# Head softmax: GpSimd's order of issue, weighing and quarter sums, and ScalarE's copy of eight heads behind the unit's own second exponential

## The chip, the cores and the metric

One core of a Trainium2 chip runs the whole program. The metric is the device time in microseconds of one execution; runs of this kernel are compared by their medians. Below, TensorE (PE) multiplies, VectorE (DVE) and ScalarE (ACT) work elementwise and reduce, GpSimd (POOL) does elementwise work and issues some DMAs, SyncE (SP) issues the other DMAs.

## What is computed

One transformer-like block on x of 4 x 1024 tokens by 128 features: banded attention, a mixture-of-experts feed-forward, then the attention of this case, and the feed-forward again. The attention of this case takes its softmax over the heads (axis 1), not over the keys:

```python
def _L0_attn_b_ref(x, Wq, bq, Wk, bk, Wv, bv, Wo, bo):
    B, S, E = x.shape
    H = N_HEADS          # 16
    D = E // H           # 8
    q = (x @ Wq.T + bq).reshape(B, S, H, D)
    k = (x @ Wk.T + bk).reshape(B, S, H, D)
    v = (x @ Wv.T + bv).reshape(B, S, H, D)
    scores = jnp.einsum('bqnd,bknd->bnqk', q, k) / jnp.sqrt(jnp.float32(D))
    attn = jax.nn.softmax(scores, axis=1)
    out = jnp.einsum('bnqk,bknd->bnqd', attn, v)
    out = out.transpose(0, 2, 1, 3).reshape(B, S, E)
    return out @ Wo.T + bo
...
x = x + _L0_attn_b_ref(_layernorm(x, axis=-1), ...)
```

So for each pair of query and key the sixteen scores are exponentiated and divided by their sum, and nothing is summed over keys but the weighted values.

## The kernel before

The stage is one function, `head_softmax_attention`. It has 4 batches of 8 query tiles (128 queries), and 8 key tiles for each query tile. One query tile against one key tile is a **unit**: 256 of them, in order. Each engine has its own program for the whole stage, a plain loop over the units written out by hand, and runs its instructions strictly in that order; semaphores alone tie the engines together. A unit's scores are [128 keys, 16 heads x 128 queries], held in PSUM in two halves of 64 queries (h = 0 and 1), two banks each. A half's banks are used again by the next unit's same half.

What one unit does, with the lines of the kernel before:

- TensorE makes the scores of a half (L890) and VectorE takes their maximum over the heads, negated (L1115, `head_shift`). TensorE adds it to the scores in place (L912, semaphore `shifted`), and ScalarE takes the exponential of the half into `ex` (L1069), a ring of 6 units.
- The sum over the 16 heads goes by halving. ScalarE copies heads 0 to 7 of the unit's `ex` into `half` (L1032, `copy_heads`). GpSimd issues a DMA that adds heads 8 to 15 onto them in place (L847, `add_halves`, 512 KB counted read and written). GpSimd adds heads 4 to 7 onto 0 to 3 (L853, `add_quarters`). TensorE sums the last four by four matmuls with the identity (L922, `denominator_of`) into the bank `den`; the profile shows them as eight.
- ScalarE turns the denominator into its reciprocal by a logarithm (L1038) and two exponentials: `recp` in PSUM for VectorE (L1041) and `recip` in SBUF for GpSimd (L1043). VectorE weighs the first ten heads (L1122), GpSimd the other six (L859, `weigh_rest`).
- TensorE multiplies the weighed exponentials with the values, 16 matmuls by head, 32 in the profile (L905, `attend`).

The denominator of unit u - 4 is made while unit u's scores are, and unit u - 5 is attended to in the same turn. TensorE's order in a turn is: maximum matmul of (u, 0), scores of (u, 1), denominator of u - 4, scores of (u + 1, 0), maximum matmul of (u, 1), attend to u - 5, and then extra work by key tile (`ahead`): with key tile 0 the next query tile's projection, with 2 the keys and with 4 the values of the next batch, with 6 the output product of the query tile before (L928, L929). The scores of a half wait for the exponential that last read its banks. VectorE's order: reduction of (u, 1), of (u + 1, 0), weighing of u - 4, and extra work: with key tile 1 the low part of the queries (L1102), with 3 that of the keys (L1102), with 5 the values, with 7 the residual sum, with 0 and 2 statistics. ScalarE's order in a turn is: first exponential, copy of unit u - 1, with key tile 5 the copy of the attention's result (L1048), the three instructions of the reciprocal of u - 4, second exponential, and with key tile 1 and 3 the high part of queries and keys (L1027), for which L1102 waits. The keys, and values, of a next batch are made in the first three batches alone.

GpSimd's loop has one step a turn, with s its number: weigh unit s - 4, issue the DMA of unit s - 1, add the quarters of unit s - 2. The DMA waits for the copy, the quarters for the DMA's landing, the weighing for `recip`.

`exps` and `copies` give the value that the semaphore `ex_ready` has when an exponential or a copy is done; all three kinds of ScalarE's instructions raise it in their order.

Of the kernel before, what the change touches and what calls it, by code (L numbers as in the profile page):

```python
# [715 lines left out]
def head_softmax_attention(nc, c, x, mv, ht, q_dram, k_dram, k_first, zero_f16, zero_f32):  # L716
# [8 lines left out]
    LAG, RING, SUMS = 4, 6, 4  # L725
    ON_DVE = 10
    BY_DMA = 0
    ALL = B * NQ * BT
# [4 lines left out]
    with Mem(nc, "head") as m:  # L733
# [34 lines left out]

        def exps(unit, h):

            return 3 * unit + 2 if h == 1 else max(3 * unit, 1)

        def copies(unit):

            return 3 * unit + (4 if unit < ALL - 1 else 3)

        def turned(k):

            return (den, recp, outp)[k % 3]

        def chunks(eng, chunk_of):

            for b in range(B):
                chunk_of(b, 0, 0)
                for pair in range(0, (NQ - 2) // 2):
                    chunk_of(b, pair * 2 + 1, 1)
                    chunk_of(b, pair * 2 + 2, 0)
                chunk_of(b, NQ - 1, 1)

        def is_chunk(b, q, n):  # L790

            return isinstance(q, int) and b * NQ + q == n
# [47 lines left out]
        @block.gpsimd  # L840
        def _(pool):
            m.start(pool, "pool")

            def add_halves(unit):

                pool.wait_ge(ex_ready, ONE + copies(unit))
                pool.dma_start(half[:, unit % SUMS, :, :], ex[:, unit % RING, 8:16, :], accum_op=ALU.add).then_inc(summed[unit % 2], 16)  # L847

            def add_quarters(unit):

                pool.wait_ge(summed[unit % 2], (unit // 2 + 1) * 16)
                hf = half[:, unit % SUMS, :, :]
                pool.tensor_tensor(hf[:, 0:4, :], hf[:, 0:4, :], hf[:, 4:8, :], ALU.add).then_inc(quarter_ready, 1)  # L853

            def weigh_rest(unit):

                pool.wait_ge(copy_ready, ONE + unit + 1)
                e = ex[:, unit % RING, ON_DVE:NH, :]
                pool.tensor_tensor(e, e, recip[:, unit % 2, :][:, None, :].broadcast_to([P, NH - ON_DVE, P]),  # L859
                                   ALU.mult).then_inc(rest_ready, 1)  # L860

            for step in range(ALL + LAG):
                if step >= LAG:
                    weigh_rest(step - LAG)
                if 0 < step <= ALL:
                    add_halves(step - 1)
                if 1 < step <= ALL + 1:
                    add_quarters(step - 2)

        @block.tensor  # L870
        def _(pe):
# [141 lines left out]
        @block.scalar  # L1013
        def _(act):
            m.start(act, "act")
            act.wait_ge(rstd_chain, ONE + 1)
            act.activation(std[:, :], std[:, :], ACT.Sqrt).then_inc(std_ready, 1)
            act.preload_act_table_set("natural_log_exp_and_others")

            def high_turned(k):  # L1020

                act.wait_ge(turned_ready, ONE + k + 1)
                act.activation(xnT[:, 0, k * BLK:(k + 1) * BLK], turned(k)[:, :], ACT.Copy).then_inc(xhigh_ready, 1)

            def high_part(parts, bank, cols, u):

                return act.activation(parts, bank[:, None, :].broadcast_to([P, 2, cols]), ACT.Identity, bias=c["b_bias"][:, u:u + 1])  # L1027

            def copy_heads(unit):

                act.wait_ge(ex_ready, ONE + exps(unit, 1))
                act.activation(half[:, unit % SUMS, BY_DMA:8, :], ex[:, unit % RING, BY_DMA:8, :], ACT.Copy).then_inc(ex_ready, 1)  # L1032

            def reciprocal_of(unit):

                act.wait_ge(copy_ready, ONE + unit)
                act.wait_ge(den_ready, ONE + unit + 2)
                act.activation(lnd[:, :], den[:, 0:P], ACT.Ln).then_inc(ln_done, 1)  # L1038
                act.wait_ge(ln_done, ONE + unit + 1)
                act.wait_ge(prob_ready, ONE + unit + 1)  # L1040
                act.activation(recp[:, 0:P], lnd[:, :], ACT.Exp, scale=-1.0).then_inc(recip_ready, 1)  # L1041
                act.wait_ge(rest_ready, ONE + unit)
                act.activation(recip[:, unit % 2, :], lnd[:, :], ACT.Exp, scale=-1.0).then_inc(copy_ready, 1)  # L1043

            def copy_out(n):
                act.wait_ge(av_done, ONE + n * BT + BT + RING - 1)
                act.wait_ge(out_ready, ONE + n)
                act.activation(outT[:, :], outp[:, 0:P], ACT.Copy).then_inc(outT_ready, 1)  # L1048

            def ahead(b, q, kt):  # L1050
                n = b * NQ + q
                if kt == 1 and not is_chunk(b, q, LAST):
                    act.wait_ge(q_ready, ONE + n + 2)
                    act.wait_ge(q_written, ONE + (n + 1) * 16)
                    high_part(parts_q[:, 0:3:2, :], proj[:, at_q], P, 0).then_inc(q_high, 1)
                if kt == 3 and b < B - 1:
                    act.wait_ge(k_ready, ONE + n + HALVES + 1)
                    act.wait_ge(k_written, ONE + (n + HALVES) * 16)
                    high_part(parts_k[:, 0:2, :], proj[:, at_k], P, 1).then_inc(k_high, 1)

            def chunk_of(b, q, par):
                n, first = b * NQ + q, is_chunk(b, q, 0)
                for kt in range(BT):
                    unit = n * BT + kt
                    for h in range(2):
                        act.wait_ge(shifted, ONE + 2 * unit + h + 1)
                        if h == 0:
                            act.wait_ge(av_done, ONE + unit)
                        act.activation(ex[:, unit % RING, :, h * QS:(h + 1) * QS].rearrange("p (a g) w -> p g a w", g=NG),  # L1069
                                       score[:, h, :, :].rearrange("p k (g a w) -> p (k g) a w", a=GH, w=QS),  # L1070
                                       ACT.Exp, scale=SCALE / ASCALE ** 2).then_inc(ex_ready, 1)
                        if h == 0 and unit > 0:
                            copy_heads(unit - 1)
                        if h == 0 and kt == LAG + 1 and not first:
                            copy_out(n - 1)
                        if h == 0 and not (first and kt < LAG):
                            reciprocal_of(unit - LAG)
                    ahead(b, q, kt)

            high_turned(0)  # L1080
            high_turned(1)
            for i in range(HALVES):
                act.wait_ge(k_ready, ONE + i + 1)
                high_part(parts_first[:, i, 0:2, :], score[:, 0, i, :], BLK, 1).then_inc(k_high, 1)
                if i == 0:
                    act.wait_ge(q_ready, ONE + 1)
                    high_part(parts_q[:, 0:3:2, :], score[:, 1, 0, 0:P], P, 0).then_inc(q_high, 1)
            for k in range(2, NBLK):
                high_turned(k)
            chunks(act, chunk_of)  # L1090
            copy_heads(ALL - 1)
            for kt in range(BT - LAG, BT):
                reciprocal_of(LAST * BT + kt)
            copy_out(LAST)
# [690 lines left out]
```

## Time and profile before

| | us |
|---|---|
| three runs | 1952.0, 1943.28, 1948.12 |
| their median | 1948.12 |
| the profiled execution's own time | 1951.87 |
| its span, first to last instruction | 1950.1 |
| busy in it: TensorE matmuls | 1835.9 (94%) |
| VectorE | 1653.7 (85%) |
| ScalarE | 1434.7 (74%) |
| GpSimd | 1443.5 (74%) |
| first and last exponential of the stage start at | 547.8, 1619.0 |
| granted clock of TensorE, 548 to 580 | 0.74 of full |
| the same, 900 to 934, 1200 to 1234 and 1500 to 1534 | 1.00 |

The shares are means over four stages with different limits, and the head softmax stage is a little over half of the span. Busy shares don't say what it waits for, since four engines are above 85% in it. The timeline does: it gives the start of each instruction, and two starts on one engine or on two are a link whose length can be read. A bracket at a row's end says how long the engine was idle before it and what released it. Instructions of one engine often overlap a little (the end of one lies behind the start of the next), so links are best measured from start to start. PE is the matmul itself, PEld the loading of its weights.

### The profile page before, as it was taken

Reading aid. Unit: us, or ns where it says so; the run is one execution under the profiler, and the core shown is the slowest. Engines: PE = TensorE matmul, PEld = TensorE weight load, DVE = VectorE, ACT = ScalarE, POOL = GpSimd, SP = SyncE. Lnnn points to the kernel's source line nnn. Section 1 sums busy time; section 2 is a strip of 40 time slices with the busy share of each in tenths; the row PEclk is TensorE's granted clock in tenths of the full one; section 3 lists DMA queues with packets and bytes.
Section 4 is the critical chain, followed back from the end, with each engine's and each line's share of the span. In section 5 each row is a group of like instructions: output and inputs, shape, how many; then the busy total and the mean of one; then the engine's idle time right before and its main releaser. Section 6 shows DMA issues by size and latency. Waiting matters only on the chain. (4 is left out here: it accounts for less than half of the span.)

```text
span 1950.1 us, 52397 instructions
## 1 busy us (share of the span) xinstructions
PE 1835.9 (94%) x20664; PEld 1154.3 (59%) x20664; DVE 1653.7 (85%) x2601; ACT 1434.7 (74%) x2473; POOL 1443.5 (74%) x1180
## 2 busy tenths in 40 slices
PE   5999799999789999999999999999999997999998
PEld 3666644444346666666666666666666665544443
DVE  6777688887679999999999999999999995788776
ACT  4566456666568888888888888888888884566665
POOL 6245256565349999999999989989999997456565
PEclk8999699999879999999999999999999997899999
DMA  6644176765267777777777667777767772677673
GB/s 162 195 110 105 27 150 140 135 141 113 81 140 141 143 136 140 136 139 139 139 136 142 133 134 144 139 136 139 137 125 138 135 134 56 130 151 154 124 133 56
DMA packets 156741, 253.07 MB, mean 130 GB/s; under 512 B 54736, under 2 KB 86368, under 8 KB 155760
## 3 DMA queue, kind: packets, MB, share of 16 engines
q0 software_dynamic: 36864, 134.23, 36.7%
q1 hardware_dynamic: 114112, 112.89, 26.7%
q8 instruction: 164, 2.69, 0.6%
q10 hardware_dynamic: 5520, 2.60, 0.5%
q14 instruction: 81, 0.66, 0.1%
HBM read 96.95 MB, written 18.55 MB: 59 GB/s over the span
## 5 line engine op out<-in xcount | busy, mean ns | idle before, releaser
L1115 DVE TENSOR_REDUCE head_shift<-head_score 128x64 bf16<-128x1024 f32 x512 | 625.8, 1222 | 74.4 <-PE head_score L890 48.2
L1069 ACT ACTIVATE head_ex<-head_score 128x1024 f32<-128x1024 f32 x512 | 521.1, 1018 | 121.5 <-PE head_score L912 120.9
L859 POOL TENSOR_TENSOR head_ex<-head_ex,head_recip 128x768 f32<-128x768 f32 x256 | 491.0, 1918 | 7.3 <-ACT head_recip L1043 6.6
L1371 POOL TENSOR_TENSOR ffn_sw<-ffn_sg,ffn_wide 128x512 f32<-128x512 f32 x256 | 324.9, 1269 | 218.4 <-ACT ffn_sg L1482 203.7
L853 POOL TENSOR_TENSOR head_half<-head_half 128x512 f32<-128x512 f32 x256 | 359.4, 1404 | 70.1 <-DMA head_half<-head_ex 67.8
L1122 DVE TENSOR_TENSOR head_ex<-head_ex,head_recp 128x1280 f32<-128x1280 f32 x256 | 378.2, 1477 | 10.0 <-ACT head_recp L1041 10.0
L912 PE MATMUL head_score<-head_shift,c_identb 128*128 128x512 bf16 x1024 | 311.7, 386 | 17.0 <-DVE head_shift L1115 11.7
L890 PE MATMUL head_score<-att_b_HB,att_b_GR 96*128 96x256 f16 x2048 | 312.4, 275 | 1.4 <-ACT head_ex L1069 1.4
L922 PE MATMUL head_den<-head_half,c_ident 128*128 128x128 f32 x2048 | 281.6, 281 | 20.2 <-POOL head_half L853 19.3
L847 POOL DMA_DIRECT2D head_half<-head_ex x256 | 251.2, 981 | 47.3 <-ACT head_half L1032 47.3
L905 PE MATMUL head_outp<-head_ex,att_b_vs 128*32 128x128 f32 x8192 | 277.4, 277 | 0.0
L922 PEld LDWEIGHTS head_den<-head_half,c_ident 128*128 128x128 f32 x2048 | 251.6, 193 | 39.4 <-POOL head_half L853 36.1
L905 PEld LDWEIGHTS head_outp<-head_ex,att_b_vs 128*32 128x32 f32 x8192 | 210.2, 110 | 107.0 <-issue 106.7
L1032 ACT ACTIVATE head_half<-head_ex 128x1024 f32<-128x1024 f32 x256 | 268.6, 1049 | 0.0
L1616 DVE TENSOR_TENSOR ffn_hidden<-ffn_sw,ffn_up 128x512 f32<-128x512 f32 x256 | 178.2, 696 | 93.1 <-POOL ffn_sw L1371 86.6
L1482 ACT ACTIVATE ffn_sg<-ffn_gate 128x512 f32<-128x512 f32 x272 | 162.4, 597 | 115.8 <-PE ffn_gate L116 114.7
L890 PEld LDWEIGHTS head_score<-att_b_HB,att_b_GR 96*128 96x128 f16 x2048 | 189.0, 98 | 88.2 <-ACT head_ex L1069 40.1
L1487 ACT ACTIVATE ffn_h_parts<-ffn_hidden 128x512 f16<-128x512 f32 x272 | 162.5, 597 | 97.4 <-DVE ffn_hidden L1616 90.6
L1624 DVE TENSOR_TENSOR ffn_h_parts<-ffn_hidden,ffn_h_parts 128x512 f16<-128x512 f32 x272 | 186.0, 684 | 0.1
L912 PEld LDWEIGHTS head_score<-head_shift,c_identb 128*128 128x128 bf16 x1024 | 66.9, 98 | 107.7 <-DVE head_shift L1115 83.9
L114 PE MATMUL ffn_down<-ffn_h_parts,c_down_parts 128*128 128x512 f16 x272 | 103.2, 379 | 3.3 <-DVE ffn_h_parts L1624 3.3
L114 PE MATMUL ffn_up<-ffn_xnT,c_up_parts 128*128 128x512 f16 x272 | 104.0, 382 | 0.6 <-DVE ffn_hidden L1616 0.3
(265 smaller groups left out, 2538.7 us busy)
## 6 DMA issues: line engine op xcount, KB each, us to landing
head_half<-head_ex POOLq DMA_DIRECT2D x256, 512.0 KB, 5.0
ffn_wide<-pair_weights SPq DMA_DIRECT2D x256, 256.0 KB, 9.7
band_v_windows<-a_values SPq DMA_DIRECT2D x24, 192.0 KB, 4.8
att_b_vs<-in_zero_f SPq DMA_DIRECT2D x2, 2176.0 KB, 10.0
a_keys<-band_parts_k SPq DMA_DIRECT2D x12, 295.5 KB, 2.5
att_a_HB<-a_keys SPq DMA_DIRECT2D x48, 73.9 KB
a_queries<-band_parts_q SPq DMA_DIRECT2D x12, 271.5 KB, 2.9
att_a_GR<-a_queries SPq DMA_DIRECT2D x12, 271.5 KB
```

The costliest lines, as they stand in the source:

```text
L847: pool.dma_start(half[:, unit % SUMS, :, :], ex[:, unit % RING, 8:16, :], accum_op=ALU.add).then_inc(summed[unit % 2], 16)
L853: pool.tensor_tensor(hf[:, 0:4, :], hf[:, 0:4, :], hf[:, 4:8, :], ALU.add).then_inc(quarter_ready, 1)
L859: pool.tensor_tensor(e, e, recip[:, unit % 2, :][:, None, :].broadcast_to([P, NH - ON_DVE, P]), ALU.mult).then_inc(rest_ready, 1)
L890: last = pe.matmul(score[:, h, g // 2, (g % 2) * GH * QS:(g % 2 + 1) * GH * QS].rearrange("p (a w) -> p a w", a=GH), GR[:, buf, g, kt * P: ...
L905: last = pe.matmul(outp[g * 32:(g + 1) * 32, 0:P], vs[:, buf * BT + kt, at:at + 32], ex[:, unit % RING, i, :], start=(kt == 0 and n4 == 0) ...
L912: last = pe.matmul(score[:, h, k, :].rearrange("p (a w) -> p a w", a=NH // 2), c["identb"][:, :], shift[:, h, :][:, None, :].broadcast_to( ...
L922: last = pe.matmul(den[:, 0:P], c["ident"][:, :], half[:, unit % SUMS, k, :], start=(i == 0), stop=(i == len(SLABS) - 1))
L1032: act.activation(half[:, unit % SUMS, BY_DMA:8, :], ex[:, unit % RING, BY_DMA:8, :], ACT.Copy).then_inc(ex_ready, 1)
L1069: act.activation(ex[:, unit % RING, :, h * QS:(h + 1) * QS].rearrange("p (a g) w -> p g a w", g=NG), score[:, h, :, :].rearrange("p k (g a ...
L1115: dve.tensor_reduce(shift[:, h, :], score[:, h, :, :].rearrange("p k (a w) -> p w k a", a=NH // 2), AX.XY, ALU.max, negate=True).then_inc( ...
L1122: dve.tensor_tensor(e, e, recp[:, 0:P][:, None, :].broadcast_to([P, ON_DVE, P]), ALU.mult).then_inc(prob_ready, 1)
L1371: pool.tensor_tensor(sw[:, unit % 2, :], sg[:, unit % 2, :], wide[:, k % 2, i, :], ALU.mult).then_inc(sw_ready, 1)
```

## The change

ScalarE's copy of a unit's heads 0 to 7 moves: from behind the first exponential of the next unit to behind the second exponential of its own unit, ahead of the `ahead` work and of the next unit's first exponential. The counts in `exps` and `copies` follow that order, and the last unit's separate copy goes. GpSimd's step is now: issue the DMA of unit s - 1, weigh unit s - 4, add the quarters of unit s - 2. At its end the last unit's quarters come ahead of the last three weighings. Nothing else is changed; no instruction is added or taken away.

```diff
         def exps(unit, h):
 
-            return 3 * unit + 2 if h == 1 else max(3 * unit, 1)
+            return 3 * unit + h + 1
 
         def copies(unit):
 
-            return 3 * unit + (4 if unit < ALL - 1 else 3)
+            return 3 * unit + 3
...
-            for step in range(ALL + LAG):
+            for step in range(ALL + 1):
+                if step > 0:
+                    add_halves(step - 1)
                 if step >= LAG:
                     weigh_rest(step - LAG)
-                if 0 < step <= ALL:
-                    add_halves(step - 1)
-                if 1 < step <= ALL + 1:
+                if step > 1:
                     add_quarters(step - 2)
+            add_quarters(ALL - 1)
+            for unit in range(ALL + 1 - LAG, ALL):
+                weigh_rest(unit)
...
-                        if h == 0 and unit > 0:
-                            copy_heads(unit - 1)
+                        if h == 1:
+                            copy_heads(unit)
                         if h == 0 and kt == LAG + 1 and not first:
                             copy_out(n - 1)
                         if h == 0 and not (first and kt < LAG):
...
             chunks(act, chunk_of)
-            copy_heads(ALL - 1)
             for kt in range(BT - LAG, BT):
```

ScalarE, around the units with key tile 0 to 2 of a query tile, before. `head_ex` is written by the exponentials (L1069), `head_half` by the copy (L1032), `head_parts_q` is the high part of the queries; x2 stands for a second exponential and the next unit's first:

```order
L1069 ACTIVATE head_ex<-head_score 128x4x4x64 x2
L1032 ACTIVATE head_half<-head_ex 128x1024
L1038 ACTIVATE head_lnd<-head_den 128x128
L1041 ACTIVATE head_recp<-head_lnd 128x128
L1043 ACTIVATE head_recip<-head_lnd 128x128
L1069 ACTIVATE head_ex<-head_score 128x4x4x64
L1027 ACTIVATE head_parts_q<-head_proj,c_b_bias 128x2x128
L1069 ACTIVATE head_ex<-head_score 128x4x4x64
L1032 ACTIVATE head_half<-head_ex 128x1024
L1038 ACTIVATE head_lnd<-head_den 128x128
L1041 ACTIVATE head_recp<-head_lnd 128x128
```

And with the change (there the lines are L1072 for the exponentials, L1035 for the copy, L1041, L1044 and L1046 for the reciprocal, L1030 for the parts):

```order
L1035 ACTIVATE head_half<-head_ex 128x1024
L1072 ACTIVATE head_ex<-head_score 128x4x4x64
L1041 ACTIVATE head_lnd<-head_den 128x128
L1044 ACTIVATE head_recp<-head_lnd 128x128
L1046 ACTIVATE head_recip<-head_lnd 128x128
L1072 ACTIVATE head_ex<-head_score 128x4x4x64
L1035 ACTIVATE head_half<-head_ex 128x1024
L1030 ACTIVATE head_parts_q<-head_proj,c_b_bias 128x2x128
L1072 ACTIVATE head_ex<-head_score 128x4x4x64
L1041 ACTIVATE head_lnd<-head_den 128x128
L1044 ACTIVATE head_recp<-head_lnd 128x128
L1046 ACTIVATE head_recip<-head_lnd 128x128
```

The copy has gone from behind the first of two adjacent exponentials to between them, and the parts of the queries stand behind it.

GpSimd, the end of its loop, before (L847 is the DMA, L859 the weighing, L853 the quarters, here and with the change; a step began with L859):

```order
L859 TENSOR_TENSOR head_ex<-head_ex,head_recip 128x768
L847 DMA head_half<-head_ex 128x1024
L853 TENSOR_TENSOR head_half<-head_half 128x512
L859 TENSOR_TENSOR head_ex<-head_ex,head_recip 128x768
L853 TENSOR_TENSOR head_half<-head_half 128x512
L859 TENSOR_TENSOR head_ex<-head_ex,head_recip 128x768 x2
```

And with the change:

```order
L853 TENSOR_TENSOR head_half<-head_half 128x512
L847 DMA head_half<-head_ex 128x1024
L859 TENSOR_TENSOR head_ex<-head_ex,head_recip 128x768
L853 TENSOR_TENSOR head_half<-head_half 128x512 x2
L859 TENSOR_TENSOR head_ex<-head_ex,head_recip 128x768 x3
```

The DMA stands ahead of the weighing instead of behind it; at the end two quarter sums are adjacent and three weighings follow them, where before the last quarter sum had a weighing ahead of it and two behind.

## Rows read from the trace of the kernel before

**Rows 1.** The line of the exponentials: durations in ns, first and last start.

```profile
L1069 ACT ACTIVATE head_ex<-head_score x512: 1002/1025/1028, 547.8 to 1619.0; 128x1024 f32<-128x1024 f32 x171
```
**Rows 2.** Timeline, 920 to 926.5, a unit with key tile 1; start, duration, engine.

```profile
920.20 0.59 PE L912 MATMUL head_score<-head_shift,c_identb 128*128 128x512 bf16 x2
...
920.83 1.02 ACT L1069 ACTIVATE head_ex<-head_score 128x1024 f32<-128x1024 f32 x1 [0.69 <-PE head_score L912]
...
921.05 0.29 DVE L1132 BATCH_NORM_STATS2 head_stats<-x_tokens 128x6 f32<-128x128 f32 x1
...
921.27 2.56 DVE L1115 TENSOR_REDUCE head_shift<-head_score 128x64 bf16<-128x1024 f32 x2
...
921.75 1.05 ACT L1032 ACTIVATE head_half<-head_ex 128x1024 f32<-128x1024 f32 x1
...
921.96 0.60 PE L890 MATMUL head_score<-att_b_HB,att_b_GR 96*128 96x256 f16 x4
...
922.55 0.60 PE L912 MATMUL head_score<-head_shift,c_identb 128*128 128x512 bf16 x2
...
922.70 0.27 ACT L1038 ACTIVATE head_lnd<-head_den 128x128 f32<-128x128 f32 x1
...
923.42 1.00 ACT L1069 ACTIVATE head_ex<-head_score 128x1024 f32<-128x1024 f32 x1
...
923.74 1.48 DVE L1122 TENSOR_TENSOR head_ex<-head_ex,head_recp 128x1280 f32<-128x1280 f32 x1
...
924.10 0.60 PE L912 MATMUL head_score<-head_shift,c_identb 128*128 128x512 bf16 x2
...
924.32 0.46 ACT L1027 ACTIVATE head_parts_q<-head_proj,c_b_bias 128x256 f16<-128x256 f32 x1
...
924.47 0.39 PEld L890 LDWEIGHTS head_score<-att_b_HB,att_b_GR 96*128 96x128 f16 x4 [0.26 <-ACT head_ex L1069]
...
925.13 0.34 DVE L1102 SCALAR_TENSOR_TENSOR head_parts_q<-head_proj,c_b_bias,head_parts_q 128x128 f16<-128x128 f32 x1
```
**Rows 3.** Timeline, 910.5 to 916: the output product, and scores that came late.

```profile
910.98 0.49 PE L928 MATMUL head_proj<-c_b_bo,c_ident 128*128 128x128 f32 x2
...
911.53 0.59 PE L912 MATMUL head_score<-head_shift,c_identb 128*128 128x512 bf16 x2
...
913.82 0.60 PE L890 MATMUL head_score<-att_b_HB,att_b_GR 96*128 96x256 f16 x4
...
914.26 0.60 PE L912 MATMUL head_score<-head_shift,c_identb 128*128 128x512 bf16 x2
...
914.46 1.23 DVE L1115 TENSOR_REDUCE head_shift<-head_score 128x64 bf16<-128x1024 f32 x1 [0.64 <-PE head_score L890]
...
915.60 1.48 DVE L1122 TENSOR_TENSOR head_ex<-head_ex,head_recp 128x1280 f32<-128x1280 f32 x1
```
**Rows 4.** Waits, 580 to 1616: engine, line, releaser; total, times, longest.

```profile
POOL head_half L853 <- DMA head_half<-head_ex: 67.2, 87, 2.0
...
PEld head_den L922 <- POOL head_half L853: 28.8, 62, 1.6
...
PE head_den L922 <- POOL head_half L853: 13.1, 26, 1.3
```
**Rows 5.** GpSimd's quarters (durations in ns, min/median/max) and the landing of L847's DMA.

```profile
L853 POOL TENSOR_TENSOR head_half<-head_half x256: 1257/1377/1592, 559.8 to 1630.0; 128x512 f32<-128x512 f32 x128
...
DMA to landing us min/median/max: 4.5/5.0/6.9
```
**Rows 6.** Timeline, 1618.5 to 1641: the end of the stage.

```profile
1618.97 1.00 ACT L1069 ACTIVATE head_ex<-head_score 128x1024 f32<-128x1024 f32 x1
...
1620.01 1.06 ACT L1032 ACTIVATE head_half<-head_ex 128x1024 f32<-128x1024 f32 x1
...
1631.37 2.07 PE L922 MATMUL head_den<-head_half,c_ident 128*128 128x128 f32 x8 [1.62 <-POOL head_half L853]
...
1633.37 6.08 PE L905 MATMUL head_outp<-head_ex,att_b_vs 128*32 128x128 f32 x160
```
## The prediction

> **Words.** A unit is one key tile against one query tile; there are 256, eight to a query tile, and I number the eight 0 to 7. "First" and "second" mean the two halves of a unit (h = 0, 1). "Maximum matmul" is L912 (it adds the negated maximum to the scores), "scores" L890, "reduction" L1115, "copy" L1032, "quarters" L853, "parts" L1027 with VectorE's L1102. Every link below is a start-to-start time in us.
>
> **What bounds the kernel now.** The change touches only the head softmax stage, so I read first how long that takes: its 512 exponentials run from 547.8 to 1619.0 [rows 1], and with 2.6 between a unit's two exponentials (923.42 - 920.83) [rows 2] the 255 steps take 1068.6, 4.19 a unit, 33.52 for eight. Then the timeline of a unit in which nothing waited for GpSimd [rows 2]: from first maximum matmul to the next unit's, 920.20 to 924.10, is 3.90. This is a loop of TensorE and VectorE: second scores, the reduction at 921.27, the second maximum matmul 1.28 after it at 922.55, the weighted sum, and round. ScalarE is not in it: its first exponential starts 0.63 behind the matmul that releases it, then copy, logarithm, two reciprocals, second exponential. Units 0, 2, 4 and 6 have extra TensorE work (0.55 for the output product, 911.53 - 910.98) [rows 3]; units 0, 1, 3, 5 and 7 have extra VectorE work (0.22: 921.27 - 921.05) [rows 2]. What is left of the 4.19 is read from the waits: the denominator's matmul waited 13.1 for GpSimd's quarters and its weight load 28.8 [rows 4], partly the same waits, and GpSimd itself 67.2 in 87 waits for the DMA that adds the upper heads. So the loop bounds, GpSimd's lateness adds to it, and ScalarE has room, but only where its work stands now.
>
> **What the change removes.** The copy of a unit ends behind the same unit's second exponential, and GpSimd issues its DMA before it weighs. A unit's DMA then goes out nearly a unit earlier, and the quarters have one weighing more to wait behind. The landing takes 4.5 to 6.9, 5.0 in the middle [rows 5], and now has over a step of GpSimd for it. I take all waits of rows 4 for gone: worth 13.1 at the least (the matmul's own) and 28.8 at the most. The Trainium skill ("DMA: Bandwidth & Descriptors", section "Anatomy of one DMA — SWDGE (gpsimd) path") gives 2.0 us and 436 KB per us, which for these 512 KB would be an estimate of 3.2; were that so, the 87 waits would not be there and this term would be nought. The trace has 5.0, so the term stays.
>
> The tail gains too. The last copy starts at 1620.01 and takes 1.06 [rows 6], 5.0 for the DMA [rows 5] and 1.38 for the quarters [rows 5] bring the last denominator to 1627.45 instead of 1631.37: 3.9 less, since 160 matmuls wait behind it (1633.37). GpSimd's three last weighings now stand behind these quarters, but TensorE reaches their units one after another in 6.08, so I cost them at nothing; were that cover gone, about a weighing each would come back.
>
> **What the change adds: a new loop.** The copy now stands between a unit's second exponential and the next unit's first. The first question is room: the two maximum matmuls that release these exponentials are 1.55 apart (924.10 - 922.55) [rows 2]. The copy needs its own exponential finished: behind the last one it started 1.04 later (1620.01 - 1618.97) [rows 6], where an instruction that needs nothing of its predecessor starts 0.92 later (921.75 - 920.83) [rows 2]. And 0.95 after the copy the next can start (922.70 - 921.75). That is 1.99 where there is 1.55: the next first exponential is 0.44 late, and only 0.08 of that is free, since the scores that wait for it start at 921.96 and it can be read 1.05 after its start (924.47 - 923.42), at 921.88. The second exponential, freed of the copy ahead of it, does start earlier, but only until its own matmul's 0.63.
>
> So a loop through ScalarE closes, from second maximum matmul to second maximum matmul: 0.63 to the exponential, 1.04 to the copy, 0.95 to the next first exponential, 1.05 to the scores that overwrite its bank, 0.44 to the maximum matmul behind them (914.26 - 913.82) [rows 3]. Sum **4.11**, against 3.90.
>
> The Trainium skill ("Perfetto Trace Analysis", section "Per-engine timelines") says that an instruction on ScalarE may begin when the one ahead has finished executing, while its semaphore moves only after memory has acknowledged the bytes. The trace agrees, 0.92 against 1.04. Had the copy started after 0.92, the loop would be 3.99 and the final sum about 8 less.
>
> Where the parts are made (unit 1 for queries; unit 3 for keys, in the first three of four batches: 32 - 1 and 24 times, 55 in all), they stand behind the copy on ScalarE, and VectorE's L1102 waits for them. Now VectorE takes it right behind its weighing (925.13, 1.39 after 923.74) [rows 2]. Then: 0.63 + 1.04 + 0.95, 0.46 for the parts, 0.05 to hand over (924.47 is 0.05 behind the end of the exponential, 923.42 + 1.00), 0.22 on VectorE, 1.28 to the maximum matmul: **4.63**. The next reductions are queued behind that waiting instruction, and TensorE waits for them.
>
> Where VectorE has extra work (units 5, 7, 0) the late scores meet it: 0.64 from scores to second reduction (914.46 - 913.82), 1.14 to the weighing (915.60), 1.39, 0.22, 1.28, less the 0.44 from scores to maximum: **4.23**. Unit 6, with the output: 3.90 + 0.55 = **4.45**, above the ScalarE loop. Units 2 and 4: 4.11.
>
> **The sum.** Eight units: 2 x 4.63 + 3 x 4.23 + 4.45 + 2 x 4.11 = 34.62. In the last batch, without keys and values, units 3 and 5 fall to 4.11: 33.98. Before: 33.52. So 24 query tiles lose 1.10 and 8 lose 0.46: 30.1. The waits on the quarters are inside the 33.52 and are not in the new sum, so their gain is already counted. Less 3.9 at the end: +26.2. The profiled execution took 1951.87, which makes 1978.1; against the median of the runs, 1948.12, it makes **1974**. Other stages don't change.
>
> **Rivals.**
> A, faster: the lateness of the first exponential is swallowed, the waits on the quarters go. For it: TensorE has the denominator's matmuls to do before those scores. Against it: 0.08 of cover where 0.44 is needed [rows 2]. It decides once the copy needs under 1.63 in all. It gives 13.1 + 3.9 = 17 to 28.8 + 3.9 = 33 less: 1931 to 1915; I take 1925. The Trainium skill's 3.2 for the DMA (same page and section, an estimate) would leave it the tail alone.
> B, nothing: ordinary units swallow it, in part because quarters no longer push TensorE, and only the 55 units with parts pay 4.63 - 4.11 = 0.52, 28.6 in all. With the gains of A this is +12 to -4, in the middle 1952.
> C, slower still: the chain lengthens and something keeps the denominator late as well, so that the 13.1 isn't won: 1987 (with the 28.8, 2003). Against it: quarters would be done almost a unit before they are needed.
> That the change doesn't do what it says (a DMA no earlier, because GpSimd now waits for the copy) is part of C; the copy ends 1.0 into the next unit, while GpSimd comes to it later.
>
> **Chances.** Forecast 0.58; A 0.18; B 0.14; C 0.10. The runs can tell about 0.5%, 10 us, from no change. Forecast and C are slower by more; of B 0.11 lie within and 0.03 above; of A 0.17 are faster and 0.01 within. Faster 0.17, same 0.12, slower 0.71. The range runs from 1950, the middle of B, to 1995, between the two prices of C: 0.58 + about half of B + most of C, the forecast's own errors included (its links are read to 0.01 to 0.05, and 0.05 in a link that every unit has is 13 us).
>
> **What would show it.** Right: 4.3 a unit between first exponentials; the copy about 1.04 behind the second exponential, the first exponential with no idle time ahead of it, mostly 0.95 behind the copy; GpSimd's 67.2 for the DMA and TensorE's waits for quarters near nought; in their place TensorE waiting for the exponential, VectorE waiting for scores (more than before), and L1102 waiting for ScalarE some 0.5 in units 1 and 3; the last denominator 6.4 behind the end of the last copy. Wrong: first exponentials that still follow their matmul by 0.63 with scores on time (A); L1102 alone late (B); waits on quarters still there (C).

## The result, and the profile after

The changed kernel takes 1984.65 us (median of 4 runs, 1983.31 to 1985.94) against 1949.37 for the kernel before in the same comparison: a ratio of 1.0191, 95% interval 1.0165 to 1.0218. It is slower by 35 us. The two profiled spans are 1950.1 and 1982.5, 32.4 apart. The forecast was 1974, in a range of 1950 to 1995.

The waits of the kernel after, from 580 to 1650 (engine, line, what it waited for; us in total, times, longest). In its numbering the exponentials are L1072, the copy L1035, the maximum matmul L915, the scores L893, the denominator L925, the reduction L1117, VectorE's low part L1104, GpSimd's weighing L859:

```profile
POOL head_ex L859 <- ACT head_recip L1046: 104.2, 186, 1.0
PEld head_score L893 <- ACT head_ex L1072: 98.7, 217, 0.8
...
DVE head_shift L1117 <- PE head_score L893: 64.8, 194, 0.5
...
PE head_score L893 <- ACT head_ex L1072: 52.7, 141, 0.6
ACT head_lnd L1041 <- PE head_den L925: 11.4, 31, 0.4
DVE head_parts_q L1104 <- ACT head_parts_q L1030: 11.3, 30, 0.5
...
DVE head_parts_k L1104 <- ACT head_parts_k L1030: 7.4, 23, 0.3
```

Nothing in it waits for GpSimd's quarters or for its DMA any more, where [rows 4] had 67.2, 28.8 and 13.1. In their place TensorE's scores wait for the exponential that reads their banks, 52.7 by the matmul itself. Before, the same view (580 to 1616) had no such wait of the matmul, and for its weight load

```profile
PEld head_score L890 <- ACT head_ex L1069: 34.6, 118, 0.4
```

GpSimd now waits for ScalarE instead of the DMA: it has become early.

The line of the exponentials, which answers to [rows 1] (durations in ns, first and last start):

```profile
L1072 ACT ACTIVATE head_ex<-head_score x512: 1002/1023/1028, 548.1 to 1656.9; 128x1024 f32<-128x1024 f32 x171
```

It spans 1108.8 where it spanned 1071.2: the stage's loop alone is 37.6 longer. What stands behind the last exponential got shorter, so the loss is all in the loop.

Two turns of the loop after, in order of time (start, duration, engine). The first is a unit with key tile 1, as in [rows 2]:

```profile
974.75 0.60 PE L915 MATMUL head_score<-head_shift,c_identb 128*128 128x512 bf16 x2
...
975.39 1.03 ACT L1072 ACTIVATE head_ex<-head_score 128x1024 f32<-128x1024 f32 x1 [0.28 <-PE head_score L915]
...
976.45 1.06 ACT L1035 ACTIVATE head_half<-head_ex 128x1024 f32<-128x1024 f32 x1
...
977.41 0.46 ACT L1030 ACTIVATE head_parts_q<-head_proj,c_b_bias 128x256 f16<-128x256 f32 x1
977.76 1.01 ACT L1072 ACTIVATE head_ex<-head_score 128x1024 f32<-128x1024 f32 x1
977.90 0.35 DVE L1104 SCALAR_TENSOR_TENSOR head_parts_q<-head_proj,c_b_bias,head_parts_q 128x128 f16<-128x128 f32 x1 [0.38 <-ACT head_parts_q L1030]
978.17 2.54 DVE L1117 TENSOR_REDUCE head_shift<-head_score 128x64 bf16<-128x1024 f32 x2
...
978.83 0.61 PE L893 MATMUL head_score<-att_b_HB,att_b_GR 96*128 96x256 f16 x4 [0.60 <-ACT head_ex L1072]
...
979.44 0.61 PE L915 MATMUL head_score<-head_shift,c_identb 128*128 128x512 bf16 x2
```

From second maximum matmul (974.75) to the next (979.44) are 4.69: 0.64, 1.06, 0.96 on ScalarE, 0.49 to L1104, 0.27, 1.27. VectorE stood idle 0.38 for the parts, TensorE 0.60 for the exponential. The second turn is one with key tile 5, without parts:

```profile
992.46 0.60 PE L915 MATMUL head_score<-head_shift,c_identb 128*128 128x512 bf16 x2
...
993.09 1.03 ACT L1072 ACTIVATE head_ex<-head_score 128x1024 f32<-128x1024 f32 x1 [0.24 <-PE head_score L915]
...
994.15 1.06 ACT L1035 ACTIVATE head_half<-head_ex 128x1024 f32<-128x1024 f32 x1
...
995.12 1.00 ACT L1072 ACTIVATE head_ex<-head_score 128x1024 f32<-128x1024 f32 x1
...
996.18 0.61 PE L893 MATMUL head_score<-att_b_HB,att_b_GR 96*128 96x256 f16 x4 [0.24 <-ACT head_ex L1072]
...
996.67 0.61 PE L915 MATMUL head_score<-head_shift,c_identb 128*128 128x512 bf16 x2
```

Here the loop closes through ScalarE: 0.63 to the exponential, 1.06 to the copy, 0.97 to the next first exponential, 1.06 to the scores that wait for it, 0.49 to the maximum matmul, 4.21. ScalarE's first exponential has no idle time ahead of it; before, it had 0.69.

The loop has also become quite regular. The parts of the queries come once in eight units; on ScalarE they start at 907.91, 942.66 and 977.41, which is 34.75 and 34.75 apart. Before, eight units took 33.5 in the mean and anything between 32.8 and 34.7.

The end of the stage, to be held against [rows 6]:

```profile
1657.99 1.06 ACT L1035 ACTIVATE head_half<-head_ex 128x1024 f32<-128x1024 f32 x1
...
1664.46 1.26 POOL L853 TENSOR_TENSOR head_half<-head_half 128x512 f32<-128x512 f32 x1 [0.67 <-DMA head_half<-head_ex]
...
1666.07 1.91 PE L925 MATMUL head_den<-head_half,c_ident 128*128 128x128 f32 x8 [0.52 <-ACT head_lnd L1041]
...
1667.91 4.57 PE L908 MATMUL head_outp<-head_ex,att_b_vs 128*32 128x128 f32 x160
...
1672.55 0.28 ACT L1051 ACTIVATE head_outT<-head_outp 128x128 f32<-128x128 f32 x1 [3.65 <-PE head_outp L908]
```

From the last exponential (1656.93) to the copy of the result (1672.55) are 15.62; before they were 20.56 (1618.97 to 1639.53). That is 4.9 gained.

### The profile page after: what moved, and what is told of

Its sections match the earlier page's. It is cut to its first block and busy times, and to the rows that moved or that the text cites. A ratio compares the mean times of both kernels' runs of the same rounds, so it can differ in the third digit from the quotient of the medians.

```text
span 1982.5 us, 52397 instructions
## 1 busy us (share of the span) xinstructions
PE 1838.1 (93%) x20664; PEld 1163.1 (59%) x20664; DVE 1656.9 (84%) x2601; ACT 1471.1 (74%) x2473; POOL 1435.8 (72%) x1180
## 5 line engine op out<-in xcount | busy, mean ns | idle before, releaser
L1117 DVE TENSOR_REDUCE head_shift<-head_score 128x64 bf16<-128x1024 f32 x512 | 625.2, 1221 | 88.1 <-PE head_score L893 75.0
L1072 ACT ACTIVATE head_ex<-head_score 128x1024 f32<-128x1024 f32 x512 | 520.7, 1017 | 104.2 <-PE head_score L915 104.0
L859 POOL TENSOR_TENSOR head_ex<-head_ex,head_recip 128x768 f32<-128x768 f32 x256 | 467.7, 1827 | 111.9 <-ACT head_recip L1046 107.5
L893 PE MATMUL head_score<-att_b_HB,att_b_GR 96*128 96x256 f16 x2048 | 315.2, 277 | 62.0 <-ACT head_ex L1072 56.7
L853 POOL TENSOR_TENSOR head_half<-head_half 128x512 f32<-128x512 f32 x256 | 326.0, 1274 | 0.7 <-DMA head_half<-head_ex 0.7
L915 PE MATMUL head_score<-head_shift,c_identb 128*128 128x512 bf16 x1024 | 312.3, 387 | 3.9 <-DVE head_shift L1117 3.7
L893 PEld LDWEIGHTS head_score<-att_b_HB,att_b_GR 96*128 96x128 f16 x2048 | 181.6, 98 | 182.0 <-ACT head_ex L1072 107.9
L925 PE MATMUL head_den<-head_half,c_ident 128*128 128x128 f32 x2048 | 273.1, 277 | 4.2 <-POOL head_half L853 3.7
L1035 ACT ACTIVATE head_half<-head_ex 128x1024 f32<-128x1024 f32 x256 | 270.8, 1058 | 8.1
L908 PE MATMUL head_outp<-head_ex,att_b_vs 128*32 128x128 f32 x8192 | 275.9, 276 | 0.0
L908 PEld LDWEIGHTS head_outp<-head_ex,att_b_vs 128*32 128x32 f32 x8192 | 208.3, 110 | 106.6 <-issue 106.5
L847 POOL DMA_DIRECT2D head_half<-head_ex x256 | 221.8, 866 | 53.6 <-ACT head_half L1035 50.3
L925 PEld LDWEIGHTS head_den<-head_half,c_ident 128*128 128x128 f32 x2048 | 250.8, 193 | 8.2 <-POOL head_half L853 4.9
L915 PEld LDWEIGHTS head_score<-head_shift,c_identb 128*128 128x128 bf16 x1024 | 74.0, 98 | 70.5 <-DVE head_shift L1117 59.1
```

The lines of the kernel that those rows point to most:

```text
L893: last = pe.matmul(score[:, h, g // 2, (g % 2) * GH * QS:(g % 2 + 1) * GH * QS].rearrange("p (a w) -> p a w", a=GH), GR[:, buf, g, kt * P: ...
L908: last = pe.matmul(outp[g * 32:(g + 1) * 32, 0:P], vs[:, buf * BT + kt, at:at + 32], ex[:, unit % RING, i, :], start=(kt == 0 and n4 == 0) ...
L915: last = pe.matmul(score[:, h, k, :].rearrange("p (a w) -> p a w", a=NH // 2), c["identb"][:, :], shift[:, h, :][:, None, :].broadcast_to( ...
L925: last = pe.matmul(den[:, 0:P], c["ident"][:, :], half[:, unit % SUMS, k, :], start=(i == 0), stop=(i == len(SLABS) - 1))
L1117: dve.tensor_reduce(shift[:, h, :], score[:, h, :, :].rearrange("p k (a w) -> p w k a", a=NH // 2), AX.XY, ALU.max, negate=True).then_inc( ...
```

## The experiments

The theory (S) is the forecast's: the copy's new place closes a loop through ScalarE that every unit pays, and more where parts stand behind the copy; GpSimd's new order only takes waits away. Rival G: GpSimd's order is what costs. Rival P: only the 55 units with parts cost, the others swallow the copy. All ratios are against the kernel before, run beside each on the same chip (median 1949.47 us beside the first four runs below, 1950.04 beside the last two).

**One part each.** The first kernel is the one before with GpSimd's new loop alone:

```diff
-            for step in range(ALL + LAG):
+            for step in range(ALL + 1):
+                if step > 0:
+                    add_halves(step - 1)
                 if step >= LAG:
                     weigh_rest(step - LAG)
...
+            add_quarters(ALL - 1)
+            for unit in range(ALL + 1 - LAG, ALL):
+                weigh_rest(unit)
```

The second is the one before with the new place of the copy alone, with the counts in `exps` and `copies` that go with it and without the last unit's separate copy (not shown):

```diff
-                        if h == 0 and unit > 0:
-                            copy_heads(unit - 1)
+                        if h == 1:
+                            copy_heads(unit)
```

> GpSimd's new order (issue, weigh, quarters last) with ScalarE's copy where it was before. Theory S (the copy's place closes a loop through ScalarE; GpSimd's order only takes waits away): the waits for quarters vanish, 4.12 us a unit instead of 4.19, the tail 4 to 5 us shorter, together 1926 us. Rival G (GpSimd's order is what costs: its weighing now stands behind a DMA that waits for the copy, so six heads are weighed late): about as slow as the change, 1985. Rival P (only the 55 units with parts behind the copy cost) expects the same as S here.

Measured: 1930.31 us, ratio 0.9914 (0.9891 to 0.9937). Its line of the exponentials, and GpSimd's quarters with what they waited for and who waited for them:

```profile
L1072 ACT ACTIVATE head_ex<-head_score x512: 1002/1023/1026, 546.8 to 1600.0; 128x1024 f32<-128x1024 f32 x171
```

```profile
L853 POOL TENSOR_TENSOR head_half<-head_half x256: 1263/1561/2507, 558.7 to 1608.2; 128x512 f32<-128x512 f32 x128
its engine sat idle before it (us, times) until:
  DMA head_half<-head_ex: 0.7, 1
who waited for it (us, times):
  PEld head_den L925: 5.6, 3
```

The loop is 1053.2 long instead of 1071.2, 18 less, which is 4.12 a unit as expected. The DMA wait, 67.2 before from 580 to 1616, is 0.7 in the whole stage, and TensorE waits for quarters only at the very end. The tail is 18.04 (1599.99 to 1618.03) instead of 20.56: 2.5, not 4 to 5, of the gain. GpSimd's order gains; G is out for this half.

> ScalarE's copy behind the unit's own second exponential, GpSimd in its order of before. S: the loop as slow as with the whole change, 34.75 us for eight units, since the quarters have time enough in the longer turn; the tail as before, so 1985 + 5 = 1990 us. G: no slower than before, 1949 or less. P: 1990 as well.

Measured: 1989.2 us, ratio 1.0216 (1.019 to 1.0242). Its exponentials and its wait for the DMA:

```profile
L1069 ACT ACTIVATE head_ex<-head_score x512: 1002/1024/1027, 548.9 to 1657.5; 128x1024 f32<-128x1024 f32 x171
```

```profile
  DMA head_half<-head_ex: 31.7, 56
```

The loop is 1108.6 long; the whole change has 1108.8. So with the copy in its new place GpSimd's order no longer moves the loop, though GpSimd still waits 31.7 for DMAs in the old order: the longer turn covers it. What the order does then is to shorten the tail from 20.05 to 15.62. Alone each half is -19 and +40; together they are +35 and not +21, because the 18 that GpSimd's order is worth in the loop can't be had behind a slower loop.

**The length of the copy.** The forecast says that copy and hand-over need 1.99 of ScalarE where 1.63 would be swallowed. Taking the copy to half its heads should bring it under that:

```diff
...
+            pool.memset(half[:, :, 4:8, :], 0.0).then_inc(half_clear, 1)
+            pool.wait_ge(half_clear, ONE + 1)
             for step in range(ALL + 1):
...
-                act.activation(half[:, unit % SUMS, BY_DMA:8, :], ex[:, unit % RING, BY_DMA:8, :], ACT.Copy).then_inc(ex_ready, 1)
+                act.activation(half[:, unit % SUMS, 0:4, :], ex[:, unit % RING, 0:4, :], ACT.Copy).then_inc(ex_ready, 1)
```

> The change, but ScalarE copies 4 heads instead of 8 (GpSimd clears the other four once at the start of the stage, so the denominator leaves out work and is not the reference's). The copy should take about 0.6 instead of 1.06 us, so that copy and hand-over need some 1.55 us against the 1.63 that are free. S: the loop through ScalarE falls to about 3.7 and no longer bounds; TensorE and VectorE bound at 4.12, 1928 us. P: units with parts still pay, 0.52 x 55 less 0.43 x 55, about 1935. G: no effect, 1985.

> Control for the run before it: the kernel before with the same four-head copy (and the same part of the denominator left out). S: the copy is not on the path there, so at most a few us: 1944 to 1950 us. If it gains as much as the four-head copy does in the change, the copy's length was binding in both and its place is not the cause.

Measured: 1937.15 us in the change, ratio 0.9948 (0.9927 to 0.9969), and 1949.16 in the kernel before, ratio 1.0004 (0.9987 to 1.0021). A turn without parts of the first of the two (L1075 is the exponential, L1038 the copy, L918 the maximum matmul):

```profile
905.58 1.03 ACT L1075 ACTIVATE head_ex<-head_score 128x1024 f32<-128x1024 f32 x1 [0.15 <-PE head_score L918]
...
906.48 0.60 PE L918 MATMUL head_score<-head_shift,c_identb 128*128 128x512 bf16 x2
906.63 0.63 ACT L1038 ACTIVATE head_half<-head_ex 128x512 f32<-128x512 f32 x1
...
907.17 1.00 ACT L1075 ACTIVATE head_ex<-head_score 128x1024 f32<-128x1024 f32 x1
```

From second to first exponential are 1.59 (1.05 and 0.54), against 2.03 in the turn at 993.09 of the change. That is under the 1.63, and the exponential comes 0.69 behind its matmul instead of the usual 0.63. 47 us of the change's time are gone; the same shortening in the kernel before is worth nothing. So it is the copy in that place, not the copy's length as such. The run stays 7 us above the kernel with GpSimd's order alone, which S had at nothing, so that P's 1935 lies nearer to it than S's 1928. What is left is in the units with parts, where 0.36 stands between copy and exponential. The scores still waited 9.3 us for the exponential, in 53 waits: 30 behind the parts of the queries and 23 behind those of the keys, and none elsewhere.

```profile
PE head_score L896 <- ACT head_ex L1075: 9.3, 53, 0.2
```

**The parts.** The change with `copy_heads(unit)` moved from ahead of `ahead(b, q, kt)` to behind it:

```diff
-                        if h == 1:
-                            copy_heads(unit)
                         if h == 0 and kt == LAG + 1 and not first:
                             copy_out(n - 1)
                         if h == 0 and not (first and kt < LAG):
                             reciprocal_of(unit - LAG)
                     ahead(b, q, kt)
+                    copy_heads(unit)
```

> The change, with the parts of queries and keys ahead of the copy on ScalarE instead of behind it, in 55 units. S (the copy's place costs in every unit, and more where parts stand behind it): these units fall from 4.63 to 0.63 + 0.92 + 0.42 + 0.95 + 1.05 + 0.44 = 4.41 us, 12 less in all, 1973 us, and L1102 no longer waits for ScalarE. Rival P (the whole loss was in these 55 units, the others swallow the copy): about 1949. If nothing changes, the links of units 1 and 3 were put together wrongly.

Measured: 1968.94 us, ratio 1.0094 (1.0059 to 1.013); 15.7 less than the change, 12 expected. ScalarE in a unit with key tile 1:

```profile
968.38 1.02 ACT L1072 ACTIVATE head_ex<-head_score 128x1024 f32<-128x1024 f32 x1 [0.29 <-PE head_score L915]
969.30 0.47 ACT L1030 ACTIVATE head_parts_q<-head_proj,c_b_bias 128x256 f16<-128x256 f32 x1
969.65 1.06 ACT L1035 ACTIVATE head_half<-head_ex 128x1024 f32<-128x1024 f32 x1
970.60 1.02 ACT L1072 ACTIVATE head_ex<-head_score 128x1024 f32<-128x1024 f32 x1
```

2.22 between the exponentials instead of 2.37 (975.39 to 977.76): the parts start 0.92 behind the exponential because they need nothing of it, and the copy then has its input ready. P is out: 19 of the 35 us stay when the parts no longer wait. These units now turn in 4.38, 4.41 expected, and nothing waits for the parts any more. S holds in both its terms.

**A version that beats both.** GpSimd's order alone is faster than both kernels. I took the loop of TensorE and VectorE for what bounds it, with VectorE a little late from its extra work in units 0, 2 and 4. So I gave GpSimd one more head to weigh:

```diff
-    ON_DVE = 10
+    ON_DVE = 9
```

> GpSimd's new order alone, and VectorE weighs 9 heads, GpSimd 7 (10 and 6 before). With the quarters on time the loop of TensorE and VectorE is what is left, 3.91 a unit, and VectorE's lateness by its extra work in units 0, 2, 4 (0.15, 0.22, 0.16 us). The weighing of 9 heads should take 0.13 less, so up to 0.4 us of 33.05 for eight units, 32 times: 13 us less than that kernel's 1930, 1917. GpSimd gets 0.3 us more a unit and has about 0.4 free; if it has less than that, its quarters or its weighing come late and the time is 1930 or more.

Measured: 1952.25 us, ratio 1.001 (0.9993 to 1.0026), 22 slower than the kernel it was made from. GpSimd's weighing (durations in ns, min/median/max), what waited for it between 600 and 1560, and one unit's values matmuls (L908):

```profile
L859 POOL TENSOR_TENSOR head_ex<-head_ex,head_recip x256: 2081/4066/4277, 567.9 to 1633.2; 128x896 f32<-128x896 f32 x128
```

```profile
PEld head_outp L908 <- POOL head_ex L859: 5.2, 33, 0.2
```

```profile
905.69 4.01 POOL L859 TENSOR_TENSOR head_ex<-head_ex,head_recip 128x896 f32<-128x896 f32 x1
...
909.03 1.36 PE L908 MATMUL head_outp<-head_ex,att_b_vs 128*32 128x128 f32 x32
```

VectorE's weighing did shrink as expected (1.34 instead of 1.48 in its rows), but GpSimd's median record went from 2.13 to 4.07 for one head more. Records on GpSimd overlap in this kernel, so their sum is not its busy time: from start to start, weighing to quarters, it is 2.06 in the median and 2.11 in the mean (2.05 to 3.25) with seven heads, 1.79 with six, and the elements alone would make 2.09. But the end of the record counts for TensorE: the weighing above ends at 909.70, and only then does TensorE load the heads that GpSimd weighed (its first weights at 909.75). The 32 matmuls take 1.2 to 1.4 in 170 of the 229 units that can be told apart in that window, where they take 1.1 in every unit of the kernel with ten heads, in which nothing waits for the weighing. Eight units take 33.5 instead of 33.05. So the seventh head costs because its weighing is done too late for TensorE. The room I saw, 0.4 a unit, was an estimate of GpSimd's free time and said nothing of when TensorE needs its result. Why a weighing is done 4.0 after its start, when the next instruction starts after 2.05, stays open.

## Why the prediction was right

**The direction and the mechanism.** The step on which all rests, that copy and hand-over need 1.99 between two exponentials whose matmuls are 1.55 apart with 0.08 to spare, held. The loop after goes round by the links that were named, and the run with a shorter copy undoes the loss while the control has none to undo. The forecast had 26 us, and the medians are 35 apart, so the loss is larger than was said.

**The links.** Predicted and measured for the turn through ScalarE: 0.63 and 0.63, 1.04 and 1.06, 0.95 and 0.97, 1.05 and 1.06, 0.44 and 0.49; 4.11 and 4.21 in the turn shown, where VectorE's extra work is a part of the last link (the forecast had 4.23 for that unit). With parts 4.63 and 4.69. The sum for eight units was 34.62 and is 34.75. Unit by unit, from second exponential to second exponential, as means over the 23 regular query tiles of the first three batches:

| unit | 0 | 1 | 2 | 3 | 4 | 5 | 6 | 7 |
|---|---|---|---|---|---|---|---|---|
| forecast | 4.23 | 4.63 | 4.11 | 4.63 | 4.11 | 4.23 | 4.45 | 4.23 |
| the change | 4.21 | 4.70 | 4.16 | 4.69 | 4.16 | 4.22 | 4.45 | 4.16 |
| GpSimd's order alone | 4.22 | 3.91 | 4.29 | 3.91 | 4.46 | 3.77 | 4.57 | 3.91 |

The links through ScalarE were read 0.05 to 0.07 too short a unit, and unit 7 has no more than the plain loop where the forecast added VectorE's extra work. The last row shows that "every unit pays" is too simple: the odd units pay (1.57 those with parts, 0.70 the other two), and the even ones give 0.56 back, since their extra work adds little or nothing to the turn now (4.16 in units 2 and 4).

**A side sum.** The prediction says that a link of 0.92 instead of 1.04 would take about 8 off. That counts units 2 and 4 alone (64 times 0.12). Its own links have the copy in the 55 units with parts too, and in units 3 and 5 of the last batch, which makes 16. The forecast doesn't use it.

**GpSimd's part.** The waits of rows 4 are gone, as forecast. That their gain is not seen in the change isn't a miss either: the sum didn't use it. The kernel with that order alone shows what it was worth, 18 us in the loop, within the 13.1 to 28.8.

**What was mis-sized.** The sum said +26.2, the spans say +32.4. To the hundredth, the loop grew by 37.7 (1108.85 less 1071.14), not by 30.1. Of the 7.6, 2.1 are in 23 query tiles, which grew by 27.4 instead of 25.3: the 0.13 in each would make 3.0, but they took 33.56 before and not the mean 33.52. The last batch grew by 6.2 instead of 3.7, which is 2.5. The other 3.0 are the first query tile: between its first exponential and the next tile's are 34.71 before and 38.78 after, 4.07 more where the sum had put 1.10 like in any other. The reason stands in the table of busy times and granted clock, before and after:

```profile
560.00:570.00 10.00, 7.85 (x40) 4.53 (x39) 5.76 (x7) 8.15 (x11) 4.61 (x5) 0.76 0.68 134
```

```profile
560.00:570.00 10.00, 8.62 (x33) 4.48 (x32) 4.78 (x6) 6.31 (x7) 3.90 (x4) 0.50 0.64 125
```

The last three columns are granted clock, DMA share and GB/s. The stage starts with TensorE at 1.2 GHz. Before, the clock is at 2.4 GHz for 3.4 us of this window, falls back, and rises for good at 568; after, it is at 1.2 GHz until 572. A turn through ScalarE at that clock, in the kernel after:

```profile
560.55 1.06 PE L915 MATMUL head_score<-head_shift,c_identb 128*128 128x512 bf16 x2
...
561.65 1.02 ACT L1072 ACTIVATE head_ex<-head_score 128x1024 f32<-128x1024 f32 x1 [1.98 <-PE head_score L915]
...
562.71 1.06 ACT L1035 ACTIVATE head_half<-head_ex 128x1024 f32<-128x1024 f32 x1
...
563.67 1.01 ACT L1072 ACTIVATE head_ex<-head_score 128x1024 f32<-128x1024 f32 x1
...
564.73 1.04 PE L893 MATMUL head_score<-att_b_HB,att_b_GR 96*128 96x256 f16 x4 [0.76 <-ACT head_ex L1072]
...
565.56 1.06 PE L915 MATMUL head_score<-head_shift,c_identb 128*128 128x512 bf16 x2
```

It takes 5.01: ScalarE's links are as ever, but the two that a matmul fills are 1.10 and 0.83 instead of the forecast's 0.63 and 0.44. The forecast's rows for the loop were all read at the full clock. At the low one the kernel before turns in 4.53 (its first three units), so here the loop through ScalarE costs at least 0.48 a unit, more with parts. The first five units together take 22.7 before and 26.3 after. GpSimd's order alone has the low clock until 566.8, all but the end of its first five units, and takes 22.8 for them; with the four-head copy in the changed kernel it is 23.3. So most of the 4.07 is the longer turn at the low clock and goes away with the shorter copy. The later rise comes on top. It was seen in all three kernels that have the full copy in its new place, 23.5 to 24.0 behind the first exponential. In three of the others and the kernel before it was 19.7 to 20.3, but in the one with nine heads 5.1, so what sets it is not settled here.

The tail gained 4.9 against 3.9. The last denominator started 7.0 behind the end of the last copy, not 6.4: the quarters start 5.4 behind it where 5.0 was put for the DMA, and the denominator waited in the end for ScalarE's logarithm of the one before it (the 0.52 in its row). But the 160 matmuls behind it ran in 4.57 instead of 6.08, at a higher granted clock (with GpSimd's order alone they took 5.80 at 0.78). Their stretch, before and after:

```profile
1633.37:1639.53 6.16, 6.08 (x161) 5.60 (x160) 1.88 (x3) 0.79 (x3) 1.83 (x1) 0.74 0.01 3
```

```profile
1667.91:1672.55 4.64, 4.57 (x161) 4.30 (x160) 1.88 (x3) 0.79 (x3) 3.16 (x2) 1.00 0.01 4
```

So 1.5 of the 4.9 are matmuls that fell into a stretch of full clock (1.00 against 0.74), which no term of the forecast had; without them the tail would have gained 3.4, less than the 3.9. That the sum came out near is in this part luck. The medians differ by 35, three more than the spans, since the kernel before scatters by 9 us from run to run.

**The rivals.** A wanted the lateness swallowed; the scores' 52.7 us for the exponential show it isn't. B wanted only the 55 units to pay; with the parts out of the way 19 us remained. C wanted late denominators; from 580 to 1650 none waited for quarters. ScalarE's logarithm waited 11.4 for denominators, 30 of the 31 times behind the output product and never over 0.4; that turn took the 4.45 that was forecast.

## What to carry to other kernels

Before moving work on an engine that is "74% busy", measure the gap that it is moved into: the time between the two events that release its neighbours, not the engine's idle share. Work between two instructions that both sit on a cross-engine loop must fit between their releases, and it pays for its own wait on the instruction ahead; work that needs something older is cheaper in the same place. And when a change has two halves, run each alone: here one half was worth 19 us and the other cost 40, and the pair hid that.

## What was not expected

Start to start on ScalarE, an instruction that needs its predecessor's result comes 1.05 to 1.06 behind a 1024-wide exponential, and one that doesn't comes 0.92 behind it; the first was known from one row of the tail alone and holds in each unit of the change. A weighing of 128 x 896 on GpSimd took 2.06 from start to start in the median, no more than its elements ask, and yet was done only 4.0 after its start, where one of 128 x 768 was done after 2.1 in the kernel with GpSimd's order alone. And the eight-unit turn, which wandered between 32.8 and 34.7 with DMA landings of 4.5 to 6.9, became constant once the landings were off the path: 22 of the 23 query tiles of the first three batches behind the first take 34.71 to 34.76.
